# The zeros of a prefix-sum scan, read from PSUM in place of SBUF, in the sort stage of a graph-network kernel

## The reference, cut to what matters

```python
# layer 1: 106250 edges, keyed by src
sums = jax.ops.segment_sum(time_feat, src, num_segments=n)
# layer 3: 106250 edges, keyed by dst (twice)
emax = jax.ops.segment_max(e, dst, num_segments=n)
denom = jax.ops.segment_sum(ex, dst, num_segments=n)
out = jax.ops.segment_sum(hp[src] * alpha[:, None], dst, num_segments=n)
# layer 4: 131072 edges, keyed by edge_index[1]
agg = jax.ops.segment_sum(msg, dst, num_segments=M)
```

## Time and profile before

| | us |
|---|---|
| median of three runs | 10350.96 |
| lowest and highest of them | 10330.89, 10361.87 |
| span of the profiled execution | 10342.3 |
| busy in it: VectorE, GpSimd | 5413.1, 5780.8 |
| busy in it: TensorE, ScalarE | 5494.0, 3566.1 |

### The profile page before, as it was taken

How to read it: one execution, slowest core, us unless ns; L and a number is a source line. 1 busy time by engine, 2 the same in 40 slices (tenths; PEclk the granted TensorE clock), 3 DMA queues, 4 the chain that set the end, 5 groups by cost and what they waited for, 6 DMA issues and landing times. The chain is left out here.

```text
span 10342.3 us, 116779 instructions
## 1 busy us (share of the span) xinstructions
PE 5494.0 (53%) x22610; PEld 3209.3 (31%) x22610; DVE 5413.1 (52%) x18917; ACT 3566.1 (34%) x11436; POOL 5780.8 (56%) x5781
## 2 busy tenths in 40 slices
PE   0000001593221149936777764777771388888897
PEld 0000000481110025523444432444441134434445
DVE  8577400492200012226666654666663287788777
ACT  0000000241000012214666642666661176666662
POOL 3787767307567740044666654666666566566650
PEclk9999975795565569967878876888885577677658
DMA  4111100010000000002333321333330111111113
GB/s 128 24 21 22 23 11 4 22 40 3 2 23 1 1 1 0 0 12 84 91 91 91 92 64 57 92 91 91 92 89 2 25 23 22 23 23 24 22 22 101
DMA packets 476242, 426.24 MB, mean 41 GB/s; under 512 B 269726, under 2 KB 409876, under 8 KB 475668
## 3 DMA queue, kind: packets, MB, share of 16 engines
q0 software_dynamic: 214016, 282.62, 11.8%
q1 hardware_dynamic: 224020, 120.13, 4.3%
q10 hardware_dynamic: 37632, 17.48, 0.7%
HBM read 341.50 MB, written 78.72 MB: 41 GB/s over the span
## 5 line engine op out<-in xcount | busy, mean ns | idle before, releaser
L449 POOL DMA_INDIRECT pay_sorted<-pay,pos x1856 | 1883.4, 1015 | 1893.7 <-PEq L1217 721.2
L790 POOL DMA_INDIRECT G<-tab_gat,pay x1856 | 1770.4, 954 | 1187.3 <-issue 465.5
L790 POOL DMA_INDIRECT G<-tab_rt,pay x1216 | 1151.5, 947 | 816.0 <-PE pLU L867 353.0
L864 PE MATMUL pU<-G,PM 128*128 128x257 f32 x3712 | 1269.6, 475 | 324.3 <-ACT PM L961 191.4
L274 POOL DMA_INDIRECT attr_sorted<-rows,pos x832 | 972.9, 1169 | 411.3 <-issue 253.4
L864 PEld LDWEIGHTS pU<-G,PM 128*128 128x128 f32 x3712 | 808.2, 241 | 485.4 <-ACT PM L961 235.6
L1679 DVE TENSOR_TENSOR t<-pO,BL 128x1024 f32<-128x1024 f32 (+1 forms) x78 | 90.7, 1163 | 1345.3 <-remote 871.0
L1078 DVE TENSOR_REDUCE mt<-pW 128x4 f32<-128x2048 f32 x304 | 695.4, 2287 | 163.5 <-issue 77.6
L810 PE MATMUL pA<-identb,G 128*20 128x128 bf16 (+1 forms) x3072 | 438.6, 250 | 477.8 <-issue 202.8
L1663 ACT ACTIVATE H<-pH,B 128x512 f32<-128x512 f32 (+1 forms) x312 | 206.6, 663 | 1364.6 <-remote 691.2
L909 ACT ACTIVATE aT<-pA 20x256 bf16<-20x256 bf16 (+1 forms) x1232 | 512.3, 416 | 457.1 <-PE pA L810 170.5
(11 more groups left out here) (324 smaller groups left out, 12213.3 us busy)
## 6 DMA issues: line engine op xcount, KB each, us to landing
pay_sorted<-pay,pos POOLq DMA_INDIRECT x1856
G<-tab_gat,pay POOLq DMA_INDIRECT x1856
G<-tab_rt,pay POOLq DMA_INDIRECT x1216
expert_parts<-pos SPq DMA_DIRECT2D x144, 128.0 KB
yl<-expert_parts SPq DMA_DIRECT2D x36, 512.0 KB, 4.0
attr_sorted<-zattr SPq DMA_DIRECT2D x1, 16896.0 KB, 53.2
rows<-attr_sorted ACTq DMA_DIRECT2D x256, 66.0 KB
attr_sorted<-rows,pos POOLq DMA_INDIRECT x832
```

What stands on the lines that cost most here:

```text
L449: pool.indirect_dma_start(out=out, out_offset=bass.IndirectOffsetOnAxis(ap=self.pos[g][:, lo + n:lo + n + 1], axis=0), in_=self.pay[g][:, ...
L790: pool.indirect_dma_start(out=G[:, j, k, 0:R], out_offset=None, in_=table, in_offset=bass.IndirectOffsetOnAxis(ap=pay[:, g % (2 * PART), k ...
L864: ins = nc.tensor.matmul(u[:, 0:F], PM[:, j % 2, k * P:(k + 1) * P], G[:, j, k, 0:F], start=(k == 0), stop=(k == K - 1))
```

## The change

A second tile of zeros, `none`, is made in PSUM (128 partitions, 1024 f32 columns, two banks), filled by one more VectorE memset at the start of the sorts, and the scan of the rank loop reads it in place of the SBUF tile `zero`. The SBUF tile stays, for the operation that presets `posf` (L396). The scan's mask and its start value still come from SBUF, and its output still goes to PSUM. Nothing else moves: on every engine the instructions stand in the order in which they stood, with the memset added on VectorE.

```diff
@@ -226,6 +226,7 @@
             posf, zero = sb("posf", [P, FT]), sb("zero", [P, FT])
             rank = ps("rank", [P, FT])
             turned = ps("turned", [1, GC * P])
+            none = ps("none", [P, FT])
@@ -342,6 +343,7 @@
                 c = Chain(dve, s_c)
                 c(v.memset(zero[:, :], 0.0))
                 c(v.memset(z49[:, :], 0.0))
+                c(v.memset(none[:, :], 0.0))
@@ -354,7 +356,7 @@
                             c(v.tensor_scalar(mm, hh, self.iota[:, bass.ds(b, 1)], None, ALU.is_equal))
-                            c(v.tensor_tensor_scan(rk, mm, zero[:, lo:hi_], base[:, bass.ds(b, 1)], ALU.add, ALU.add))
+                            c(v.tensor_tensor_scan(rk, mm, none[:, lo:hi_], base[:, bass.ds(b, 1)], ALU.add, ALU.add))
```

## The result

The kernel after takes 10449.94 us (median of 20 runs, 10367.16 to 10509.14), the kernel before 10353.12 (20 runs, 10312.97 to 10441.27): ratio 1.0083, 95% interval 1.006 to 1.0106. It is slower by 0.83%, or some 86 us (the two medians lie 97 us apart), where 10230 was forecast. The profiled execution of after took 10445.76 us with a span of 10444.0.

What follows compares the result with a forecast made beforehand. GpSimd's last scatter was taken to end the sorts, VectorE having 230 us to spare. -131.8 for the scans' hold and +11 for masks gave -121 us, so 10230 us on the median; range of 8 in 10: 10195 to 10340.

Steps and rivals of the forecast that it cites:

- Parts 1 to 4: Sorts: scans' hold on GpSimd gone, -131.8 us; masks hold scatters instead, +11; scan length unchanged, 0; added memset, 0.
- the pair of adds: Later stage: scatter under an add with two SBUF inputs takes 1.60 us, with one from PSUM 0.97.
- the 1267 of the sum: End of sorts: GpSimd would end at 1388.3 - 131.8 + 11 = 1267 us.
- the 11 us granted: Rank loops: scatters held by the mask compares would cost 11 us, with ends 0 and 32.
- D: Rank loops: reading and writing PSUM at once doubles the scan, VectorE ends at 1477 us; total 10440 us; chance 0.03.
- C: Rank loops: the scan holds GpSimd anyway, by its pointer scalar or kind; total 10351 us; chance 0.06.
- Part 5: End of sorts: VectorE's 1158 us stays 109 before GpSimd's end; longer mask waits, at most 72 us, still fit.
- rival A: Sorts: VectorE's loops turn slow, 112 more turns cost 353 us, VectorE becomes the bound; total 10474 us; chance 0.12.

Runs made afterwards that it cites:

- The spaced pair: Memset of 128x160 behind each of the 1856 later-stage scatters, in the kernel after (9427.31 us, ratio 0.9081) and in the kernel before (9376.81 us, ratio 0.9029).
- written out: Kernel after with the sorts' loops of 49 turns written out, block numbers and semaphore values constants: 10365.84 us, ratio 0.9922 to the kernel before.
- all three variants: Kernel after with the first sort's 832 scatters made gathers, landing nearly no row, or halved in rows: 10536.94, 10407.97 and 10354.88 us.

## Why the prediction was wrong

**Parts 1 to 4 held.** The scan's hold on GpSimd is gone as the pair of adds said: scatters in the slow stretches average 973 to 1051 ns, and the last one ends at 1301.4, of which 184.4 - 158.9 = 25.5 us are a wait for late positions:

```profile
POOL attr_sorted L275 <- DVE pos L403: 184.4, 2, 158.9
```

Without that it would be 1276, 9 us from the 1267 of the sum; masks and other VectorE operations take a little more than the 11 us granted. The scans last as long as before; the short ones on the path, to be laid beside the earlier trace rows:

```profile
L359 DVE TENSOR_TENSOR_SCAN rank<-mask,base,none 128x208 f32<-128x208 bf16 x49 | 32.1, 655 | 7.2 <-DVE mask L358 2.0
```

They take 655 ns in place of 658, so D is out; C is out by the scatters. The 65 ns a scan that the estimate from the Trainium skill ("VectorE: DVE Perf Modes", the section on the TRN2 errata) would have added are not there.

**Part 5 failed**: "VectorE's 1158 is still 109 us before that" took VectorE's end as given, up to 72 us of scatter contention. It was not given: it rested on the very hold that the change removes. VectorE's end went to 1465.8, which is **rival A**, named with its mechanism and given 0.12. A's price was 10474 on the median of the first three runs; the time is 10450. Its term was too large because it let all 112 further turns go slow: 113 - 35 = 78 did, 78 x 3.15 = 246 us, and slower masks and counting turns brought it to 307.7 in place of 353. That its total came out so near is in part luck: A put the whole lateness, 123 us, into the sorts and counted it from the last scatter's end at 1388, but before the change the next stage began only at 1413, after the landings. The sorts lost 55 us, and the rest arose elsewhere.

**The reason to give A only 0.12 was a misreading.** The gather loops, held up against it as "indirect DMAs at much the same pace", are not at that pace. One of them, grouped, from 4829 to 6212 us of the kernel after:

```profile
L792 POOL DMA_INDIRECT G<-tab_gat,pay x928 | 885.0, 954 | 598.4 <-issue 232.6 <-remote 171.8 <-DMA pay<-pay_sorted 101.4
```

928 in 1383 us is one per 1.49. Most come in bursts of four to six, 1.25 us apart, and from the last of a burst to the next one it is 2.6 us (median); the sorts turned slow only after 30 to 47 us of unbroken scatters, and at steady spacings of about 1.5 us they stayed quick. So these loops did not speak against A, though no run changed their own pace. The rows that spoke for A, slow turns after some 35 us of unhindered scatters and quick ones in the middle of loops that hold them, were read rightly and weighed too lightly. The place to look was the edge-sum stage of the kernel before, where the same effect stood in plain view at 30.8 us a group.

**The total.** The next stage begins at 1468.43 us in place of 1413.04 (its first memset on VectorE), 55 us later. The edge-sum stage adds nothing to that: its last ScalarE operation comes 54.6 us later. The two profiled executions part again in the adapter stage. ScalarE's 13 operations of one line there (count, ns min/median/max, first and last start), before, after, in the run that spaced the edge-sum stage alone, and in the repeat of before:

```profile
L1406 ACT ACTIVATE fu<-pB,bf x13: 362/682/683, 2413.1 to 2634.6; 64x512 f32<-64x512 f32 x12, 64x128 f32<-64x128 f32 x1
...
L1408 ACT ACTIVATE fu<-pB,bf x13: 364/684/685, 2467.6 to 2729.2; 64x512 f32<-64x512 f32 x12, 64x128 f32<-64x128 f32 x1
...
L1412 ACT ACTIVATE fu<-pB,bf x13: 362/682/683, 2116.6 to 2378.4; 64x512 f32<-64x512 f32 x12, 64x128 f32<-64x128 f32 x1
...
L1406 ACT ACTIVATE fu<-pB,bf x13: 362/682/682, 2407.3 to 2571.3; 64x512 f32<-64x512 f32 x12, 64x128 f32<-64x128 f32 x1
```

They span 222 us before and 262 after, but without the change also 262 and 164: this stage's length varies by itself. The spaced pair, with 54 us, agrees with the 55. What the remaining 30 us or so of the 86 are, no run tells.

## What to carry to other kernels

A stall on one engine can be another engine's protection. Before a stall is removed, ask what rate it kept down, find the stretches of the same trace in which that rate is already reached, and read the other engines there; an off-path engine's end isn't a constant of the sum. Where short indirect DMAs run beside work with many hand-overs, try them a little further apart: 0.2 us more for each gave 10% of this kernel, in executions that were all recorded.

## What the runs showed of the hardware

Indirect DMAs issued by GpSimd every 1.28 us slowed the other engines. In the sorts VectorE's register instructions took 691 ns in place of 57 (medians) and its turns 7.0 us in place of 3.85; written out, its semaphore updates came late and its masks and scans started at multiples of 0.70 us. In the edge-sum stage TensorE's semaphore updates came 22.7 us late (median), and groups took 30.8 us in place of 2.4. In all these stretches the trace has one semaphore update per 0.70 us, in the quick ones of the sorts, with scatters running, 10 to 14 per us. In the sorts of the kernel after, this set in 30 to 47 us after scatters ran freely and lasted 22 to 25 us after they stopped.

Direction, bytes and rows landing made no difference; the spacing did, with VectorE quick in the sorts at 1.39 us, the hand-overs of the edge-sum stage still slow at 1.41 and quick at 1.53. It is not told by any run why. What all three variants left nearly the same are the packets that GpSimd writes and the semaphore updates of each DMA. The missing updates show that the recording was at its limit in the slow stretches, and all executions were recorded; so it may be the recording itself that slows the engines. Neither fewer packets or updates per DMA at the same pace, nor a time without recording, were tried.
